# Variance products over 64 equal columns, and a GpSimd wait between the pieces of the second feed-forward matrix

## The reference

```
h = tok(x)                                   # patchify, layer norm, x W^T, layer norm, + position
h = concat(cls_tok, h)                       # 16 x 37 tokens of 256
h = h + attn0(layernorm(h))                  # 16 heads, rope, causal
h = h + moe(layernorm(h))                    # 16 experts, 74 tokens each, + shared expert
h = h + encoder(layernorm(h))                # below
h = h + fp4_ffn(layernorm(h))

def encoder(x):                              # six layers
    x = ln(x, g, b) + pos_emb
    for l in range(6):
        q, k, v = x Wq^T + bq, keys Wk^T + bk, keys Wv^T + bv     # keys: x with a past of one
        o  = softmax(mask(q k^T / 4)) v Wo^T + bo
        x  = ln(x + o, ln1_g, ln1_b)
        ff = gelu(x W1^T + b1) W2^T + b2
        x  = ln(x + ff, ln2_g, ln2_b)

def ln(x): m = mean(x); v = mean((x - m)**2); return (x - m) / sqrt(v + 1e-5)
```

## Time and profile before

| | |
|---|---|
| runs (us) | 825.94, 826.92, 830.93; median 826.92 |
| profiled execution | 826.68, of which the span from first to last instruction is 824.9 |
| granted TensorE clock, mean | 0.998 |
| PE busy | 805.6 us, 98% of the span |
| PE weight loads busy | 753.4 us, 91% |
| DVE, ACT, POOL busy | 638.5, 461.1, 254.1 us |
| one encoder layer, from one layer's start of the W1 pieces to the next's | 71.4 us (489.18 to 560.59) |

### The profile page before, as it was taken

How to read it: one execution, slowest core, us unless ns; L and a number is a source line. 1 busy time by engine, 2 the same in 40 slices (tenths; PEclk the granted TensorE clock), 3 DMA queues, 4 the chain that set the end, 5 groups by cost and what they waited for, 6 DMA issues and landing times.

```text
span 824.9 us, 16624 instructions
## 1 busy us (share of the span) xinstructions
PE 805.6 (98%) x6060; PEld 753.4 (91%) x6060; DVE 638.5 (77%) x1287; ACT 461.1 (56%) x829; POOL 254.1 (31%) x297
## 2 busy tenths in 40 slices
PE   9999999999999999999999999999999999999988
PEld 8998889999999999899989989998998999899758
DVE  5786693778778877778797887878778787876796
ACT  4386424433333345585776777667687767745421
POOL 0012120410111100364365246336525623643020
PEclk9999999999999999999999999999999999999999
DMA  5010936998898812010310021031011102020001
GB/s 189 1 52 1 383 104 253 336 321 311 306 328 320 316 48 106 1 39 14 104 39 0 20 95 38 13 102 38 5 40 70 38 13 102 14 93 1 1 0 30
DMA packets 18290, 88.36 MB, mean 107 GB/s; under 512 B 3120, under 2 KB 7472, under 8 KB 12240
## 3 DMA queue, kind: packets, MB, share of 16 engines
q1 hardware_dynamic: 18256, 87.90, 30.2%
HBM read 85.05 MB, written 2.84 MB: 107 GB/s over the span
## 4 chain that ended last, share of the span: by engine, by line
PE 50%; issue 22%; POOL 16%; DVE 10%; ACT 2%; POOLq 0%; DVEq 0%; ACTq 0%
PE bank L1138 14%; PE bank L1175 6%; POOL W_L L1999 5%; POOL HF_L L2053 4%; POOL arena L1980 4%; PE bank L722 3%; POOL WQKV_L L1999 3%; PE bank L889 2%; DVE OB L2160 2%; PE bank L1184 2%; PE bank L1048 2%; PE bank L745 2%; PE bank L787 2%; PE bank L802 2%; PE bank L904 1%
## 5 line engine op out<-in xcount | busy, mean ns | idle before, releaser
L1138 PE MATMUL bank<-arena 128*128 (+1 forms) x1024 | 117.8, 274 | 0.0
L1138 PEld LDWEIGHTS bank<-arena 128*128 128x128 f32 x1024 | 117.4, 192 | 0.0
L1980 POOL TENSOR_TENSOR arena<-arena,srec 111x456 f32<-111x456 f32 x56 | 52.4, 962 | 125.0 <-DVE srec L2148 125.0
L1999 POOL TENSOR_TENSOR W_L<-LW,W_H 128x256 fp32r<-128x256 f32 x96 | 70.9, 775 | 29.2 <-DVE XHL L2584 25.8
L2053 POOL TENSOR_TENSOR HF_L<-arena,HF_H 128x296 fp32r<-128x296 f32 x48 | 43.9, 936 | 86.5 <-ACT HF_H L1895 86.5
L787 PE MATMUL bank<-XHL,W_H 128*128 128x296 f32 x288 | 66.3, 308 | 1.2 <-DVE arena L2137 1.2
L1895 ACT ACTIVATE arena<-bank,vec 128x296 f32<-128x296 f32 x96 | 48.9, 510 | 24.6 <-PE bank L787 17.8
L2011 POOL TENSOR_TENSOR QW<-QW,arena x14 | 22.4, 1600 | 119.0 <-DVE QW L2485 65.6
L1329 PE MATMUL bank<-HF_L,W_H 128*128 128x296 f32 x192 | 57.4, 299 | 0.0
L1329 PE MATMUL bank<-HF_H,W_H 128*128 128x296 f32 x192 | 57.4, 299 | 0.0
L1329 PE MATMUL bank<-HF_H,W_L 128*128 128x296 f32 x192 | 57.3, 299 | 0.0
(11 more groups left out here) (276 smaller groups left out, 2207.1 us busy)
## 6 DMA issues: line engine op xcount, KB each, us to landing
arena<-ew_in SPq DMA_DIRECT2D x16, 2048.0 KB, 9.1
arena<-ew_in SPq DMA_DIRECT2D x16, 1024.0 KB, 6.4
LW<-lw_in SPq DMA_DIRECT2D x12, 1024.0 KB, 5.0
arena<-route SPq DMA_DIRECT2D x32, 185.0 KB, 3.3
LW<-lw_in SPq DMA_DIRECT2D x6, 768.0 KB, 4.4
fp_weights<-arena SPq DMA_DIRECT2D x1, 2048.0 KB, 6.4
arena<-fp_weights SPq DMA_DIRECT2D x1, 2048.0 KB, 7.2
arena<-patches_in SPq DMA_DIRECT2D x2, 864.0 KB, 7.8
```

The source lines that it names most:

```text
L1138: last = mm(o[:, m * CAP:(m + 1) * CAP], w[:, kc, mi * P:(mi + 1) * P], xg(kc, e), start=(kc == 0), stop=(kc == C - 1))
L1980: nc.gpsimd.tensor_tensor(v, v, srec[0:QROWS, s:s + 2, :].unsqueeze(3).to_broadcast([QROWS, 2, C * JH, KEYS]), ALU.mult).then_inc(p_ready, 1)
L1999: last = nc.gpsimd.tensor_tensor(low[:, cols], value[:, cols], high[:, cols], ALU.subtract)
```

## The change

Neither part changes what is computed.

First, the moving operand of a variance product has 64 columns of `ones_d` (or `ones_p`) instead of one. All 64 are equal, so 64 equal columns of PSUM come out; the readers take the first of each block, with a step of 64 instead of 1. The three blocks take 192 columns, and the two statistics of the patch stage move to columns 0 and 256 of their bank.

Second, POOL's eight pieces of W2 are cut into two and six, and between them POOL waits for `x_ready` of the half whose feed-forward begins, that is for DVE's `low_stream`.

```
-        VAR_AT, EX_AT, MU_AT = NHALF + 4, NHALF + 8, NHALF + 12
+        VAR_AT, VAR_W, EX_AT, MU_AT = NHALF + 4, 64, 0, 256
...
                 for t, (t0, _) in enumerate(var_tiles(nt)):
                     for c in range(nch):
-                        last = mm(ln_bank(seq, h)[:, VAR_AT + t:VAR_AT + t + 1], sq[:, h, c, t0:t0 + P], ones[:, 0:1],
+                        at = VAR_AT + t * VAR_W
+                        last = mm(ln_bank(seq, h)[:, at:at + VAR_W], sq[:, h, c, t0:t0 + P], ones[:, 0:VAR_W],
                                   start=(c == 0), stop=(c == nch - 1))
...
-                        last = mm(bank[5][:, at + t:at + t + 1], R[:, h, k, t0:t0 + P], ones_p[:, 0:1],
+                        last = mm(bank[5][:, at + t * VAR_W:at + (t + 1) * VAR_W], R[:, h, k, t0:t0 + P], ones_p[:, 0:VAR_W],
...
-                f(ln_sd[:, h, :], LNB[h][:, VAR_AT:VAR_AT + 3], ACT.Sqrt, bias=eps1[:, :]).then_inc(ln_std, 1)
+                f(ln_sd[:, h, :], LNB[h][:, VAR_AT:VAR_AT + 3 * VAR_W:VAR_W], ACT.Sqrt, bias=eps1[:, :]).then_inc(ln_std, 1)
...
                         split_part("w1", FM * P, 2 * FM * P).then_inc(wl_ready["w1"], 1)
-                        split_weights("w2", y[1])
+                        lead = 2 * LOW_COLS
+                        pool.wait_ge(wh_ready["w2"], y[1] + 1)
+                        split_part("w2", 0, lead)
+                        pool.wait_ge(x_ready, x_count(y[1], 0, 0) - skipped(y[1], 0, 0))
+                        split_part("w2", lead, 2 * FM * P).then_inc(wl_ready["w2"], 1)
```

More of the change, by code:

```diff
@@ L1566, in enc_root @@
                 act.wait_ge(ln_var, ln_count(LN_ENC, h))
-                f(ln_sd[:, h, :], ln_bank(LN_ENC, h)[:, VAR_AT:VAR_AT + 3], ACT.Sqrt, bias=eps_sq[:, :], scale=1.0 + EPS
+                f(ln_sd[:, h, :], ln_bank(LN_ENC, h)[:, VAR_AT:VAR_AT + 3 * VAR_W:VAR_W], ACT.Sqrt, bias=eps_sq[:, :], scale=1.0 + EPS
                   ).then_inc(ln_std, 1)
@@ L1593, in square_mean @@
                 act.wait_ge(patch_stats_ready, h + 1)
-                f(mean_sq[:, h, :], bank[5][:, MU_AT:MU_AT + 3], ACT.Square).then_inc(mean_squared, 1)
+                f(mean_sq[:, h, :], bank[5][:, MU_AT:MU_AT + 3 * VAR_W:VAR_W], ACT.Square).then_inc(mean_squared, 1)
             def token_root(h):
@@ L1601, in token_root @@
                 for t in range(3):
-                    last = f(ln_sd[:, h, t:t + 1], LNB[h][:, VAR_AT + t:VAR_AT + t + 1], ACT.Sqrt,
+                    last = f(ln_sd[:, h, t:t + 1], LNB[h][:, VAR_AT + t * VAR_W:VAR_AT + t * VAR_W + 1], ACT.Sqrt,
                              bias=eps_var[:, h, t:t + 1])
@@ L2244, in token_eps @@
                 dve.wait_ge(mean_squared, h + 1)
-                link(v.tensor_tensor(eps_var[:, h, :], bank[5][:, EX_AT:EX_AT + 3], mean_sq[:, h, :], ALU.subtract))
+                link(v.tensor_tensor(eps_var[:, h, :], bank[5][:, EX_AT:EX_AT + 3 * VAR_W:VAR_W], mean_sq[:, h, :], ALU.subtract))
                 v.tensor_scalar(eps_var[:, h, :], eps_var[:, h, :], EPS, EPS * EPS, ALU.mult, ALU.add
```

## The result

| | before | after |
|---|---|---|
| runs (us), seven each | 825.94 to 830.93, median 827.1 | 820.91 to 821.54, median 821.12 |
| ratio after / before | | 0.9903, 95% interval 0.9878 to 0.9928 |
| profiled execution | 826.68, span 824.9 | 820.91, span 819.1 |
| granted clock, mean of the profiled execution | 0.998 | 1.0 |

The time came out 0.2 us from the forecast of 821.3. For the gain it depends on what stands for before. The medians differ by 6.0 us (821.12 / 827.1 = 0.9928), where 5.6 us, or 0.7%, was forecast; the ratio on record, 0.9903, says 1.0%, and its interval, whose upper end is that 0.9928, shuts out no change. Most of what was misjudged lies in that spread.

What follows compares the result with a forecast made beforehand. PE was taken as the bound, busy 805.6 of 824.9 us. The sum was 826.68 - 4.3 (wait) - 1.6 (clock) + 0.3 (columns) = 821.1, with the median's 0.24 a forecast of 821.3 us; 8-in-10 range 819.9 to 825.0.

Steps and rivals of the forecast that it cites:

- The wait in GpSimd: At low_stream in six layers: holding GpSimd's pieces ends the mutual slowing with DVE, and PE gains the whole 4.3 us.
- rivals 2: At low_stream: only the first of PE's three waits goes, 1.8 us won instead of 4.3, 823.8 us; chance 0.12.
- 3: Held pieces slow other DVE instructions as much, so nothing is gained on DVE, 825.6 us; chance 0.07.
- What is late next: Ahead of down: W2's low parts end 2.4 to 3.8 us before PE needs them, so their wait costs nothing.
- Rival 4: Ahead of down, six times: W2's low parts become the bound and the kernel gets slower, 829.3 us; chance 0.04.
- The 64 columns' later landing: Variance passes: results land 0.024 us later, costing 0.3 us in 14 batches outside the encoder, nothing in the encoder's 24.
- The clock: At 87.11 to 90.52 us: wider variance products keep the granted clock from falling to 0.50, gaining 1.6 us.
- Rival 1: The clock falls again whatever the columns, only the wait in GpSimd pays, 822.9 us; chance 0.25.
- The time: Whole kernel: 821.1 us from the profiled execution, 821.3 after adding 0.24 for the median of the runs.
- The chances: Whole kernel: within 1% of before 0.91, faster by over 1% 0.06, slower by over 1% 0.03.

Runs made afterwards that it cites:

- experiment 1: The kernel before plus only GpSimd's wait, one column in every variance product: 822.15 us, ratio 0.9909 to before.
- experiment 4: The change, but with all eight pieces of W2 held behind the wait instead of six: 821.38 us, ratio 0.9904 to before.
- 9: The change with one column in all 34 norms and 64 only in the patch stage: 821.84 us, ratio 0.9890 to before.
- 11: The change run again unaltered, as base on the same chip: 821.47 us, ratio 0.9886 to before.
- 10: The change with one column in the encoder's 24 norms, 64 in the other norms and patch stage: 821.44 us, ratio 0.9887 to before.
- experiments 5: The kernel before with 64 columns only in the norm ahead of the experts, no wait, run once for its trace: 832.07 us.
- 12: The kernel before plus only GpSimd's wait, one column everywhere, run again twelve times: 827.41 us, ratio 0.9952 to before.
- experiment 6: The kernel before, unaltered, run once more for its trace: 836.29 us.
- experiment 2: The kernel before plus only the 64 columns, without GpSimd's wait: 825.73 us, ratio 0.9967 to before.
- experiment 7: The change, with GpSimd also waiting for RSUM before W1's pieces and one piece each of W1 and W2 moved later: 820.13 us, ratio 0.9887 to before.
- 8: The change with one column in the patch stage's statistics and 64 in all norms: 821.6 us, ratio 0.9888 to before.
- experiment 14: The change without the wait and with one column in all passes before 47 us: 829.52 us, ratio 0.9988 to before.

## Why the prediction was right in its parts and wrong in the gain

- **The wait in GpSimd: right.** Forecast 4.3 us. At a clock of 0.999 or 1.0, the 13 such runs among before's 74 have a median of 825.64, and the 13 runs of the change one of 821.17: 4.5 us. The same comparison for the columns alone against the change gives 825.73 - 821.17 = 4.6, for experiment 1's three undisturbed runs against before 825.64 - 821.5 = 4.1. A layer takes 70.70 us (W1's pieces start at 486.40 and 557.10), as forecast, and DVE's entries in PE's waits fell from 5.8 to 1.3 us where some 1.5 were forecast. So rivals 2 and 3 are out.
- **What is late next: right.** The held pieces end at 496.89 + 4.25 = 501.14, and `down` starts at 505.08: 3.9 us to spare, a little over the 2.4 to 3.8 estimated. Rival 4 is out, and experiment 4 shows room for two pieces more.
- **The 64 columns' later landing: the price per pass right, its effect not seen.** A pass takes 278 ns instead of 250, where 24 ns more had been taken, and ACT's wait for it is 1.4 us longer in all. The 0.3 us in the sum, for the 14 batches outside the encoder, do not show: 9, with one column in all 34 norms, is no faster than 11 (821.84 against 821.47), and the columns alone differ from before's runs at 1.0 by 0.1, between runs that scatter by 1. For the encoder's 24 nothing had been taken, and 10 against 11 differ by 0.03 us.
- **The clock: right in kind, wrong in size. This is the step that failed.** "0.41 + 0.31 + 0.92 = 1.64 us, all on the chain", and with it the level of before, "826.68 (the profiled execution)", were read from one execution with one stretch at 0.50. The traces have them at four places (31, 81 to 93, 437 and 751 us), each in some executions:

| mean clock | of before's 74 runs | median us | what a trace at that clock shows |
|---|---|---|---|
| 1.0, 0.999 | 13 | 825.64 | |
| 0.996 to 0.998 | 16 | 827.04 | one stretch of 3.41 us (before, experiment 1) |
| 0.994 | 19 | 830.12 | no trace; as much as the long stretch alone |
| 0.991, 0.992 | 24 | 832.09 | the long stretch and one short (experiments 5 and 12) |
| 0.989 | 2 | 836.10 | the long, two short, and `low_stream` held up for 4.2 us (experiment 6) |

The third and fourth rows follow from the lengths: 10.24 us at half of the clock in a span of some 825 us make a mean of 0.994, and 3.41 us more one of 0.992. The execution in hand was thus among the better ones. What the columns take away is 0 to 6.5 us in an execution; over the seven and the 74 runs together before's mean is 829.4, 3.8 us above the level of the runs at 1.0, and the term is some 3.8 us on average instead of 1.64 (experiment 2 against the runs beside it, mean against mean, gives 2.9). In 37 executions with 64 columns everywhere (the change twice, experiments 2, 4 and 7) no mean clock was under 0.999. Rival 1, in which the clock falls on, is out.
- **The time: near, and in part by luck.** The profiled execution less its clock term, 826.68 - 1.64 = 825.04, is 0.6 us below the 825.64 of before's runs at 1.0. The 0.3 us for the columns, the 0.24 added for the median and the wait's 4.5 instead of 4.3 make up for it.

- **The chances: wrong with it.** "Faster by over 1% would need a gain of 8.3 us, more than 5.8 + 1.64 from all that was found here: 0.06." Mean against mean the gain is 829.4 - 821.3 = 8.1 us; the interval reaches past 1%. The 1% itself, "about that much a measurement of this kernel can tell from no change", was too coarse: the interval is 0.25% to either side, so a change of the size that was forecast is told from none. In rival 4 the time was added up wrongly: 826.9 + 6 x 0.4 leaves out the columns' -1.6 + 0.3, with which it would be 828.0. The three runs given, 825.94, 826.92 and 830.93, had the spread in them: 5 us at one kernel, where 1.64 us explained the profiled one. The page "TensorE: Matmul & The Clock Gate" of the Trainium skill (section "HAM oscillation — how this bites in real kernels") was set against the trace with its gaps of an idle PE. The traces show both: at 437.64 the clock fell behind 3.0 us of idle PE, the kind of cause that section names; at 31.45 it fell behind none, and there the wider product ended it.

Left open: which of the front's passes (norm or patch stage) must be widened, as 8 and 9 have six runs each; why the place and the odds of a short stretch change from one execution to the next; and the 1 us by which runs at a clock of 1.0 still differ (820.0 and 821.2 in experiment 7).

## What to carry to other kernels

VectorE and GpSimd instructions that slow each other, as here where both read SBUF in the same microsecond, can be set apart by a wait on the side that has slack: here GpSimd had 4 us of it, and each VectorE instruction won back its full 0.2 to 0.5 us, as far as PE waits for it first. Before a clock term is priced from a profile, the mean clock of several executions should be set beside their times, since one trace shows one draw of the stretches. In this kernel a run of products with one moving column kept PE busy and still cost it the clock, in some executions and not in others; 64 equal columns cost 28 ns a pass, hidden here, and in 37 executions with them no mean clock was under 0.999.

## What the runs showed that was not expected

The fight between VectorE and GpSimd has a rare, long form: 4179 ns for an instruction that takes 521 alone, until GpSimd had no more pieces. The page "SBUF — State Buffer" of the Trainium skill (section "Who interferes with whom") says of the two engines that "only the shared port pair causes contention, and it's an exclusive lock". The trace agrees in that one instruction, which ended only when GpSimd had stopped; in the usual ones (745 and 998 ns in the earlier trace rows) the loss is under half a microsecond, less than one of GpSimd's pieces, and the pieces lost time too (up to 972 ns). Two of before's 74 runs and the traced one stand at 836, and two runs of experiment 14, without the wait too, stand 3 us above the others at their clock (829.0 and 833.7); no run with the wait shows such a step, though only one trace shows the cause.
